# Attention scores from two scaled float16 pieces, with pairs of heads in the two row halves of the TensorE array

## The chip, the cores and the metric

The kernel runs on one core of one Trainium2 chip. Its time is the device time of one execution in microseconds. Three runs of the kernel before gave 969.35, 967.27 and 971.53 us, median 969.35.

## The reference

The input x is 1,024 tokens by 512 features, all in float32. Four blocks follow each other, each of the form x + layernorm(f(layernorm(x))):

1. causal attention with 32 heads of 16 features, 8 groups of 4 heads; the heads of a group share keys and values. Scores are q.k / 4, the upper triangle is masked, then softmax, weighted sum, output projection and a bias;
2. a gated feed-forward layer with ternary weights and 1,792 hidden features;
3. an attention by autocorrelation over Fourier transforms, with the six largest lags;
4. a gated feed-forward layer with 1,376 hidden features and low-rank additions to its weights.

```
q = (x @ Wq).reshape(t, 32, 16);  kv = (x @ Wkv).reshape(t, 8, 2, 16)
scores = einsum('bhqd,bhkd->bhqk', q, k)          # k of head h is that of group h // 4
weights = softmax(where(causal, -inf, scores) * (1 / 16 ** 0.5))
ctx = einsum('bhqk,bhkd->bhqd', weights, v);  out = ctx @ Wo + bo
```

The change touches block 1 alone, and there the scores.

## The kernel before

**Scores in pieces.** A float32 product of q and k is made in 16-bit operands: q and k are each split into three bfloat16 pieces, and of the nine products of pieces the six in `TERMS` (L11) are kept. A head has 16 features, so six terms stack into 96 contraction rows. `qt6` holds the stacked queries of three groups of heads in a ring, with the four heads beside each other in the free dimension, `kt6` the stacked keys of all groups. Every score is computed twice. `scores` (L1306) gives tiles of 128 queries by up to 512 keys, of which VectorE takes the row maxima (`row_max`, L1217). `scores_t` (L1324) gives the same transposed, 128 keys by queries, over 99 rows: three more rows hold the negative maxima of the queries in three pieces against rows of ones in `kt6`, so that the maximum is subtracted by the matmul. ScalarE makes the exponentials of those (L1300), GpSimd masks the diagonal block (L1208), and `weighted` (L1339) sums values by weight. In `weighted` the four heads lie in four column quarters of the array, and each float32 matmul is two instructions.

**Order in a group.** A group of four heads has eight stages, one for each tile of 128 keys (`kt`). `pe_group` (L1359) writes TensorE's order out by hand. In stages 0 to 3 each head has the slots S, ST, S, ST: two score matmuls of the row tile that is 14 steps ahead (`ahead`, L1259; so of the next group, or the one after it from stage 2 on) and two halves of the transposed scores of this stage; in stages 4 to 7 it has S, ST. Some slots, by `SUM_SLOTS` (L1379), carry a part of the weighted sum of the stage before: 1, 4, 4, 3, 3, 2, 2 and 1 in the eight stages. A score matmul waits until VectorE has taken the one two before (two PSUM banks); a transposed one waits until ScalarE has taken the one two before (two double banks). After stage 1, `max_pieces` (L1240) makes the pieces of the maxima on VectorE, and SyncE transposes them and brings them into `qt6` over DRAM. `for_groups` (L1113) writes out groups 0, 6 and 7 and runs a loop over groups 1 to 5 on every engine. Group 6 has scores ahead in stages 0 and 1 alone, group 7 in none.

**Before the groups.** LayerNorm on VectorE (L1468 to L1476), 32 transposes on TensorE, then projections (L1547): j = 0 the keys, then the values, j = 1 to 4 the queries. For each projection ScalarE makes piece 0 (L1518), VectorE a remainder and pieces 1 and 2 (L1486 to L1490); SyncE stores the three and loads the stacked rows (L1397 to L1408, `load_q` L1126). The ring is refilled at the start of each group for the second one after it. Beside this run 38 jobs that add the low-rank products to the weights of block 4 (`lora_job`, L949): matmul, copy on ScalarE, addition on GpSimd, a load and a store by DMA from ScalarE's queue. Their pieces (`lora_pieces`, L512) come from VectorE between xn and the first projection's pieces. The jobs are threaded between projections and 80 score matmuls of groups 0 and 1 that are made early. The groups begin when all jobs are copied and all early scores taken.

**What the other queues hold.** GpSimd fills rows 96 to 127 of `kt6` with ones (L1446) behind the wait for x and the start of a DMA. ScalarE's queue holds the low-rank loads and stores among its copies.

## Time and profile before

| | before |
|---|---|
| median of three runs | 969.35 us |
| span of the profiled execution | 966.3 us (no separate time of it is given) |
| instructions | 14,696 |
| busy share of TensorE, VectorE, ScalarE, GpSimd | 81%, 60%, 35%, 27% |
| L1321, scores | x384, 135.0 us busy |
| L1330, transposed scores | x384, 125.7 us busy |
| L1353, weighted sums | x1280, 100.4 us busy |
| L1300, exponentials | x256, 163.4 us busy |
| L1233 and L1237, row maxima | x256 and x128, 122.0 and 88.2 us busy |
| DMA | 94.16 MB, 144,473 packets |

Busy times add up what lies side by side: matmuls are pipelined and their ends are modelled, so that the starts of consecutive matmuls say more than their durations. A window is a stretch of the span; its row gives the busy time of each engine in it and the granted clock of TensorE as a share of full speed (1.00 is 2.4 GHz, 0.50 is 1.2 GHz).

### The profile page before, as it was taken

What the parts mean: (1) busy time and instruction counts of PE and PEld (TensorE: products, weight loads), DVE (VectorE), ACT (ScalarE), POOL (GpSimd) and SP (SyncE); (2) the same over time, 40 slices, a digit from 0 to 9 for tenths busy, and PEclk for the clock granted to TensorE, in tenths of its full rate; (3) what the DMA queues carried; (4) which work ended last, traced back from release to release, by engine and by line L of the source; (5) the groups of instructions that cost most, each with busy time, mean ns of one, the idle gap of its engine ahead of it and who ended that gap; (6) DMA issues with size and microseconds to landing.
All of it is one profiled execution on the core that took longest, in us unless ns stands there. A gap on an engine that the chain in (4) does not pass through costs nothing.

```text
span 966.3 us, 14696 instructions
## 1 busy us (share of the span) xinstructions
PE 782.0 (81%) x4174; PEld 317.3 (33%) x4174; DVE 579.3 (60%) x1433; ACT 338.6 (35%) x544; POOL 261.6 (27%) x248
## 2 busy tenths in 40 slices
PE   1957667988998989887499926998757799999993
PEld 1622222222322322223244412453323344444441
DVE  7524776767677677004999998136999815722004
ACT  1122225655556456760033301447203322212220
POOL 3024452121212202321034412434301114323221
PEclk9978558999889999997889967999978899999997
DMA  9498988612312124522206667103997400201001
GB/s 267 84 194 283 263 243 205 114 27 47 67 29 45 38 48 100 94 56 79 44 13 171 200 107 218 56 1 73 149 215 148 80 9 0 44 1 44 0 1 43
DMA packets 144473, 94.16 MB, mean 97 GB/s; under 512 B 110184, under 2 KB 123368, under 8 KB 144216
## 3 DMA queue, kind: packets, MB, share of 16 engines
q1 hardware_dynamic: 133376, 71.24, 33.4%
q10 hardware_dynamic: 10816, 16.91, 5.6%
q0 software_dynamic: 240, 5.51, 2.7%
q8 instruction: 21, 0.34, 0.1%
q14 instruction: 20, 0.16, 0.1%
HBM read 49.51 MB, written 29.04 MB: 81 GB/s over the span
## 4 chain that ended last, share of the span: by engine, by line
PE 54%; DVE 16%; DMA 10%; issue 8%; SPq 5%; ACT 3%; POOL 2%; DVEq 0%; ACTq 0%; POOLq 0%
PE ps L1077 19%; PE ps L1089 8%; PE ps L1353 8%; PE ps L1321 7%; PE ps L1330 5%; PE ps L1063 5%; DVE mx L1237 3%; DMA lorad_d<-arena 2%; DMA lora_d<-arena 2%; SPq L334 2%; DMA qp_d<-arena 1%; DMA arena<-arena 1%; DVE arena L1233 1%; DVE stats L460 1%; DVE arena L500 1%
## 5 line engine op out<-in xcount | busy, mean ns | idle before, releaser
L1077 PE MATMUL ps<-arena 128*128 128x512 f16 (+1 forms) x976 | 224.7, 388 | 40.4 <-issue 22.6
L1300 ACT ACTIVATE arena<-ps 128x1024 f32<-128x1024 f32 (+7 forms) x256 | 163.4, 651 | 116.4 <-PE ps L1330 111.6
L1321 PE MATMUL ps<-arena 96*128 (+4 forms) x384 | 135.0, 377 | 37.9 <-DVE mx L1237 16.5
L1233 DVE CUSTOM_DVE_ANT_0 arena<-ps,arena 128x256 bf16<-128x256 f32 (+3 forms) x256 | 122.0, 488 | 58.1 <-PE ps L1321 50.0
L924 POOL TENSOR_TENSOR arena<-arena (+2 forms) x50 | 67.4, 1349 | 307.3 <-ACT arena L856 299.5
L1077 PEld LDWEIGHTS ps<-arena 128*128 (+2 forms) x976 | 97.7, 101 | 161.2 <-issue 54.2
L1330 PE MATMUL ps<-arena 99*128 (+4 forms) x384 | 125.7, 344 | 4.6 <-ACT arena L1300 4.2
L1089 PE MATMUL ps<-arena 128*128 (+3 forms) x488 | 114.6, 384 | 11.3 <-POOL arena L929 10.9
L1237 DVE TENSOR_REDUCE mx<-ps 128x1 f32<-128x512 f32 x128 | 88.2, 689 | 27.2 <-PE ps L1321 26.3
L1353 PE MATMUL ps<-arena 128*32 128x256 f32 (+1 forms) x1280 | 100.4, 387 | 2.8 <-POOL arena L1208 2.2
L1208 POOL TENSOR_SCALAR_AFFINE_SELECT arena<-arena 128x512 f32<-128x512 f32 x64 | 40.7, 635 | 225.5 <-ACT arena L1300 225.2
L1063 PE MATMUL ps<-arena 128*128 128x512 f16 (+1 forms) x384 | 77.7, 364 | 23.8 <-DMA arena<-arena 16.0
L1321 PEld LDWEIGHTS ps<-arena 96*128 (+1 forms) x384 | 39.2, 102 | 148.3 <-issue 78.8
L1089 PEld LDWEIGHTS ps<-arena 128*128 (+2 forms) x488 | 47.6, 98 | 72.8 <-POOL arena L929 11.8
L682 DVE TENSOR_TENSOR arena<-ps,row_b 128x512 f32<-128x512 f32 x16 | 10.8, 678 | 95.8 <-PE ps L1089 95.8
L891 POOL TENSOR_TENSOR arena<-arena 128x512 f32<-128x512 f32 (+2 forms) x38 | 43.1, 1138 | 88.0 <-ACT arena L747 49.5
L929 POOL TENSOR_TENSOR arena<-arena (+2 forms) x50 | 61.6, 1236 | 0.0
L1063 PEld LDWEIGHTS ps<-arena 128*128 128x128 f16 x384 | 38.1, 100 | 63.1 <-DMA arena<-arena 17.0
L855 ACT ACTIVATE arena<-ps,gs (+2 forms) x22 | 15.1, 687 | 123.5 <-PE ps L1077 123.4
L855 ACT ACTIVATE arena<-ps,sc (+1 forms) x28 | 19.2, 687 | 104.8 <-PE ps L1077 104.8
L1330 PEld LDWEIGHTS ps<-arena 99*128 (+1 forms) x384 | 36.5, 99 | 40.0 <-issue 15.9
L1551 PE MATMUL ps<-arena 128*128 128x512 f32 x80 | 43.2, 671 | 6.1 <-DMA arena<-arena 5.3
(144 smaller groups left out, 735.7 us busy)
## 6 DMA issues: line engine op xcount, KB each, us to landing
arena<-qp_d SPq DMA_DIRECT2D x48, 128.0 KB, 4.4
lora_d<-arena ACTq DMA_DIRECT2D x20, 256.0 KB, 4.7
arena<-lora_d SPq DMA_DIRECT2D x10, 512.0 KB, 4.2
w1n_d<-arena SPq DMA_DIRECT2D x10, 512.0 KB, 3.1
arena<-rec_d SPq DMA_DIRECT2D x32, 128.0 KB, 2.6
qp_d<-arena SPq DMA_DIRECT2D x12, 256.0 KB, 4.1
w1dn_d<-arena SPq DMA_DIRECT2D x4, 704.0 KB, 3.2
arena<-in_L_ffn_down_w_dram ACTq DMA_DIRECT2D x16, 172.0 KB, 3.4
```

The costliest lines, as they stand in the source:

```text
L924: nc.gpsimd.tensor_tensor(hs[0:h, n % 2, :], sg[0:h, n % 2, :], u_sb[0:h, n % 2, :], ALU.mult).then_inc(hs_ready, 1)
L929: nc.gpsimd.tensor_tensor(hid[0:h, 1, n % 2, :], hs[0:h, n % 2, :], hid[0:h, 0, n % 2, :], ALU.subtract).then_inc(hid_ready, 1)
L1063: last = nc.tensor.matmul(to, lhs(w, kt), rhs(r, kt), start=(kt, w, r) == (0, 0, 0), stop=(kt, w, r) == (ND - 1, 1, 0))
L1077: last = nc.tensor.matmul(ps[0:h, 2 * (n % 2) + o, :], w(t[0])[:, kt, bass.ds(ht * P, h)], xt[:, c, t[1], kt, :], start=(kt, t) == (0, ter ...
L1089: last = nc.tensor.matmul(ps[:, 4 + i, :], hid[0:h, t[0], n % 2, i * P:(i + 1) * P], down(t[1])[0:h, ht, :], start=first and t == down_ter ...
L1233: nc.vector.tensor_tensor_reduce(out=junk[:, h, 0:w], in0=s_bank(g, u)[:, 0:w], in1=strip[:, D - w:D], scale=1.0, scalar=3.0 * NEG, op0=AL ...
L1237: nc.vector.reduce_max(mx[:, h, qt:qt + 1], s_bank(g, u)[:, 0:w], mybir.AxisListType.X).then_inc(s_taken, 1)
L1300: nc.scalar.activation(probs[:, kt % 2, h, kt * P:T], st_bank(h).rearrange("p b n -> p (b n)")[:, kt * P:T], ACT.Exp, scale=HD ** -0.5).th ...
L1321: nc.tensor.matmul(s_bank(g, u)[:, 0:k1 - k0], qt6[0:QROWS, g % RING, h, qt * P:(qt + 1) * P], kt6[0:QROWS, g, k0:k1], start=True, stop=Tr ...
L1330: last = nc.tensor.matmul(st_bank(h)[:, b, q0 - b * 512:512], kt6[0:QROWS + MROWS, g, kt * P:(kt + 1) * P], qt6[0:QROWS + MROWS, g % RING, ...
L1353: last = nc.tensor.matmul(o_bank[32 * h:32 * h + 32, b, q0 - b * 512:q1 - b * 512], vcur[:, kt, :], probs[:, kt % 2, h, q0:q1], start=kt = ...
L1551: last = nc.tensor.matmul(ps[:, 2 + 2 * (j % 2) + half, :], weights(c), xnt[:, c, half * 512:(half + 1) * 512], start=c == 0, stop=c == ND ...
```

## The change

- Queries and keys are split into two float16 pieces instead of three bfloat16 pieces, and three products of pieces are kept instead of six: 48 contraction rows, 51 with the maxima. The low-rank matrices keep their six terms (`LORA_TERMS`).
- The projections are scaled by powers of two, drawn from the largest weight of Wq and of Wk: two reductions on VectorE, a matmul that turns the result, one that spreads it over the partitions, and eight small operations. The scale of the exponential is now a tile of one number per partition (`escale`).
- The four heads of a group share the array's rows: heads 0 and 1 in rows 0 to 50, heads 2 and 3 in rows 64 to 114; the keys stand in both halves. The order of the heads is (2, 0, 3, 1) for the scores and (0, 2, 1, 3) for the transposed ones; a score matmul and the transposed one behind it lie in opposite halves.
- The maxima are divided by 2^14 and the rows of ones hold 2^14. They come by two DMAs instead of one.
- VectorE makes one pass for each projection instead of three; SyncE stores two pieces instead of three. The queries of a group come by six DMAs of 64 KB (before: six of 128 KB), the keys by six of 256 KB, as before.
- The fill of `kt6` covers all of it, and stands ahead of GpSimd's wait for x; SyncE waits for it before the key loads.
- On TensorE all eight groups are written out, with no loop; the other engines keep theirs.

```diff
-TERMS = ((0, 0), (0, 1), (1, 0), (1, 1), (0, 2), (2, 0))
+TERMS = ((0, 0), (0, 1), (1, 0))
 QROWS = HD * len(TERMS)
 MROWS = 3
+HALF = P // 2
+LORA_TERMS = ((0, 0), (0, 1), (1, 0), (1, 1), (0, 2), (2, 0))
+LROWS = HD * len(LORA_TERMS)
+S_ORDER, T_ORDER = (2, 0, 3, 1), (0, 2, 1, 3)
+MAX_SHIFT = 2.0 ** 14
...
-        pc = [room(16 + 4 * i, [2, T], BF16) for i in range(3)]
-        res = room(28, [2, T])
+        pc = [room(16 + 4 * i, [2, T], F16) for i in range(2)]
-        qt6 = room(112, [RING, REP, T], BF16)
-        kt6 = room(136, [G, T], BF16)
+        qt6 = room(112, [RING, REP // 2, T], F16)
+        kt6 = room(136, [G, T], F16)
...
+        def projection_scale(j):
+
+            return wscale[:, 0:1] if j else wscale[:, 1:2]
+
+        def projection_scales(dve, link):
+
+            dve.wait_ge(wq_loaded, 16)
+            nc.vector.tensor_reduce(wtop[:, 0:1], wq.rearrange("p c n -> p (c n)"), mybir.AxisListType.X, ALU.max,
+                                    apply_absolute_value=True).then_inc(wtop_ready, 1)
+            dve.wait_ge(wk_ready, 1)
+            nc.vector.tensor_reduce(wtop[:, 1:2], wk.rearrange("p c n -> p (c n)"), mybir.AxisListType.X, ALU.max,
+                                    apply_absolute_value=True).then_inc(wtop_ready, 1)
+            dve.wait_ge(wtop_turned, 1)
+            link(nc.vector.tensor_reduce(wexp[0:2, 0:1], ps[0:2, 0, 0:P], mybir.AxisListType.X, ALU.max))
+            dve.wait_ge(ident_ready, 1)
+            nc.vector.tensor_scalar(wdiag[0:2, :], ident[0:2, 0:2], wexp[0:2, 0:1], None, ALU.mult).then_inc(wdiag_ready, 1)
+            dve.wait_ge(wtop_spread, 1)
+            link(nc.vector.tensor_copy(wexp[:, :], ps[:, 1, 0:2]))
+            exponent(link, wexp[:, :], wexp[:, :], 2.0 ** -60)
+            inverse_of(link, wscale[:, :], wexp[:, :], 2)
+            nc.vector.tensor_scalar(escale[:, :], wexp[:, 0:1], wexp[:, 1:2], HD ** -0.5 / 16,
+                                    ALU.mult, ALU.mult).then_inc(scale_ready, 1)
+            dve.wait_ge(scale_ready, 1)
...
         def load_q(sp, g):
 
-            for s, (qp, _) in enumerate(TERMS):
-                src = qp_d[qp].rearrange("(g h d) t -> g d h t", g=G, h=REP)
-                sp.dma_start(qt6[HD * s:HD * (s + 1), g % RING, :, :], src[g]).then_inc(qt_loaded, 16)
+            for r in range(2):
+                for s, (qp, _) in enumerate(TERMS):
+                    src = qp_d[qp].rearrange("(g r s d) t -> g r d s t", g=G, r=2, s=2)
+                    at = HALF * r + HD * s
+                    sp.dma_start(qt6[at:at + HD, g % RING, :, :], src[g, r]).then_inc(qt_loaded, 16)
...
-                sp.dma_start(qt6[QROWS:QROWS + MROWS, g % RING, :, :],
-                             mt_d[g, 0:MROWS * REP * NT, :].rearrange("(i r) q -> i (r q)", i=MROWS)
-                             .rearrange("i (h t) -> i h t", h=REP)).then_inc(m_loaded, 16)
+                for r in range(2):
+                    at = HALF * r + QROWS
+                    src = mt_d[g, 0:MROWS * REP * NT, :].rearrange("(i r s t) q -> r i s (t q)", i=MROWS, r=2, s=2)
+                    sp.dma_start(qt6[at:at + MROWS, g % RING, :, :], src[r]).then_inc(m_loaded, 16)
...
-            n(nc.vector.tensor_scalar(p3[:, 0], mx[:, :, :], -1.0, None, ALU.mult))
-            n(nc.vector.scalar_tensor_tensor(out=mr[:, :, :], in0=mx[:, :, :], scalar=-1.0, in1=p3[:, 0],
+            n(nc.vector.tensor_scalar(p3[:, 0], mx[:, :, :], -1.0 / MAX_SHIFT, None, ALU.mult))
+            n(nc.vector.scalar_tensor_tensor(out=mr[:, :, :], in0=mx[:, :, :], scalar=-1.0 / MAX_SHIFT, in1=p3[:, 0],
...
-                for h in range(REP):
-                    n = 32 * g + 4 * kt + h
+                for k, h in enumerate(T_ORDER):
+                    n = 32 * g + 4 * kt + k
                     act.wait_ge(st_ready, n + 1)
-                    if h == 0 and (kt >= 2 or shape > 0):
+                    if k == 0 and (kt >= 2 or shape > 0):
                         act.wait_ge(pv_done, NT * g + kt - 1)
                     nc.scalar.activation(probs[:, kt % 2, h, kt * P:T],
-                                         st_bank(h).rearrange("p b n -> p (b n)")[:, kt * P:T],
-                                         ACT.Exp, scale=HD ** -0.5).then_inc(p_ready, 1)
-                    if (kt, h) == OUT_STEP and shape > 0:
+                                         st_bank(k).rearrange("p b n -> p (b n)")[:, kt * P:T],
+                                         ACT.Exp, scale=escale[:, 0:1]).then_inc(p_ready, 1)
+                    if (kt, k) == OUT_STEP and shape > 0:
                         take_o(act, g - 1)
 
...
-            nc.tensor.matmul(s_bank(g, u)[:, 0:k1 - k0], qt6[0:QROWS, g % RING, h, qt * P:(qt + 1) * P],
-                             kt6[0:QROWS, g, k0:k1], start=True, stop=True).then_inc(s_ready, 1)
-
-        def scores_t(pe, g, kt, h, b, shape):
-
-            n = 4 * kt + h
+            rows = slice(HALF * (h // 2), HALF * (h // 2) + QROWS)
+            nc.tensor.matmul(s_bank(g, u)[:, 0:k1 - k0], qt6[rows, g % RING, h % 2, qt * P:(qt + 1) * P],
+                             kt6[rows, g, k0:k1], start=True, stop=True).then_inc(s_ready, 1)
+
...
-            last = nc.tensor.matmul(st_bank(h)[:, b, q0 - b * 512:512], kt6[0:QROWS + MROWS, g, kt * P:(kt + 1) * P],
-                                    qt6[0:QROWS + MROWS, g % RING, h, q0:q1], start=True, stop=True)
+            last = nc.tensor.matmul(st_bank(k)[:, b, q0 - b * 512:512], kt6[rows, g, kt * P:(kt + 1) * P],
+                                    qt6[rows, g % RING, h % 2, q0:q1], start=True, stop=True)
...
-                    h, half = divmod(slot, halves)
+                    k, half = divmod(slot, halves)
                     if to:
-                        scores(pe, *to, h, half, False)
-                    scores_t(pe, g, kt, h, half if halves == 2 else 1, shape)
+                        scores(pe, *to, S_ORDER[k], half, False)
+                    scores_t(pe, g, kt, k, half if halves == 2 else 1, shape)
...
-                for i in range(3):
+                for i in range(2):
                     dst = kp_d[i] if j == 0 else qp_d[i, (j - 1) * P:j * P, :]
                     sp.dma_start(dst, pc[i][:, j % 2, :]).then_inc(pieces_stored[j % 2], 16)
                 if j == 0:
-                    sp.wait_ge(pieces_stored[0], 48)
-                    for s, (_, kp) in enumerate(TERMS):
-                        sp.dma_start(kt6[HD * s:HD * (s + 1), :, :],
-                                     kp_d[kp].rearrange("(g d) t -> d g t", g=G)).then_inc(kt_loaded, 16)
+                    sp.wait_ge(pieces_stored[0], 32)
+                    sp.wait_ge(ones_ready, 1)
+                    for r in range(2):
+                        for s, (_, kp) in enumerate(TERMS):
+                            at = HALF * r + HD * s
+                            sp.dma_start(kt6[at:at + HD, :, :],
+                                         kp_d[kp].rearrange("(g d) t -> d g t", g=G)).then_inc(kt_loaded, 16)
...
+            nc.gpsimd.memset(kt6[:, :, :], MAX_SHIFT).then_inc(ones_ready, 1)
...
-            nc.gpsimd.memset(kt6[QROWS:P, :, :], 1.0).then_inc(ones_ready, 1)
-            pool.wait_ge(ones_ready, 1)
...
+            projection_scales(dve, link)
...
-                nc.vector.tensor_tensor(res[:, b, :], ps[:, 2 + 2 * b:4 + 2 * b, :].rearrange("p b n -> p (b n)"), pc[0][:, b, :],
-                                        ALU.subtract).then_inc(res_ready, 1)
-                dve.wait_ge(res_ready, j + 1)
-                link(nc.vector.tensor_copy(pc[1][:, b, :], res[:, b, :]))
-                nc.vector.tensor_tensor(pc[2][:, b, :], res[:, b, :], pc[1][:, b, :], ALU.subtract).then_inc(pieces_ready, 1)
+                nc.vector.scalar_tensor_tensor(out=pc[1][:, b, :], in0=ps[:, 2 + 2 * b:4 + 2 * b, :].rearrange("p b n -> p (b n)"),
+                                               scalar=projection_scale(j), in1=pc[0][:, b, :],
+                                               op0=ALU.mult, op1=ALU.subtract).then_inc(pieces_ready, 1)
...
-                nc.scalar.copy(pc[0][:, b, :], ps[:, 2 + 2 * b:4 + 2 * b, :].rearrange("p b n -> p (b n)")).then_inc(piece0, 1)
+                if j == 0:
+                    act.wait_ge(scale_ready, 1)
+                nc.scalar.activation(pc[0][:, b, :], ps[:, 2 + 2 * b:4 + 2 * b, :].rearrange("p b n -> p (b n)"), ACT.Copy,
+                                     scale=projection_scale(j)).then_inc(piece0, 1)
...
+            def weight_bounds(i):
+
+                if i == 0:
+                    pe.wait_ge(wtop_ready, 2)
+                    nc.tensor.matmul(ps[0:2, 0, 0:P], wtop[:, :], ident[:, :], start=True, stop=True).then_inc(wtop_turned, 1)
+                if i == 5:
+                    pe.wait_ge(wdiag_ready, 1)
+                    nc.tensor.matmul(ps[:, 1, 0:2], wones[0:2, :], wdiag[0:2, :], start=True, stop=True).then_inc(wtop_spread, 1)
+
             pe.wait_ge(wk_ready, 1)
-            project(0, lambda c: wk[:, c, :], lambda i: None)
+            project(0, lambda c: wk[:, c, :], weight_bounds)
             for t in range(NT):
...
-            pe.wait_ge(ones_ready, 1)
-            for_groups(pe, pe_group)
+            for g in range(G):
+                pe_group(pe, g, g)
```

## Rows read from the trace of the kernel before

**Rows 1.** Windows, four of the eight groups: us, busy (instructions) by engine, PEclk, DMA share, GB/s.
```profile
222.00:260.00 38.00, 33.76 (x257) 10.79 (x256) 27.35 (x86) 21.40 (x33) 7.39 (x11) 0.96 0.22 45
260.00:300.00 40.00, 36.56 (x259) 11.25 (x258) 27.51 (x87) 21.41 (x33) 8.25 (x11) 0.87 0.23 43
...
376.00:405.00 29.00, 26.70 (x225) 7.61 (x223) 11.32 (x30) 21.28 (x34) 7.74 (x11) 1.00 0.40 91
405.00:434.20 29.20, 23.58 (x214) 6.91 (x214) 0.35 (x1) 20.18 (x33) 7.79 (x11) 0.94 0.49 92
```

**Rows 2.** Windows, group 0 from stage 1 on; the last is stage 0 of group 1.
```profile
155.10:161.10 6.00, 5.93 (x49) 1.71 (x48) 4.75 (x15) 3.67 (x4) 0.90 (x3) 1.00 0.98 210
161.10:167.90 6.80, 5.23 (x49) 1.62 (x48) 5.20 (x16) 3.24 (x4) 0.60 (x1) 1.00 0.88 187
167.90:172.50 4.60, 4.43 (x40) 1.50 (x39) 3.33 (x12) 2.81 (x4) 0.67 (x2) 1.00 0.09 17
172.50:176.10 3.60, 3.60 (x34) 0.93 (x32) 2.71 (x8) 2.28 (x4) 0.60 (x1) 1.00 0.68 152
176.10:179.00 2.90, 2.69 (x25) 0.78 (x25) 2.17 (x8) 1.94 (x4) 0.64 (x2) 1.00 1.33 150
179.00:181.70 2.70, 2.31 (x27) 0.81 (x26) 1.64 (x8) 1.43 (x5) 0.66 (x2) 1.00 1.27 290
181.70:183.80 2.10, 1.88 (x16) 0.70 (x16) 1.23 (x9) 1.11 (x4) 0.62 (x2) 1.00 0.22 49
183.80:190.20 6.40, 5.64 (x27) 1.72 (x26) 5.76 (x13) 4.90 (x5) 0.67 (x2) 1.00 0.85 126
```

**Rows 3.** Timeline of TensorE: start, us, line, operands, count; key projection, then one slot.
```profile
27.11 7.13 PE L1551 MATMUL ps<-arena 128*128 128x512 f32 x16 [0.78 <-ACT arena L1508]
...
206.82 0.39 PE L1321 MATMUL ps<-arena 96*128 x1
207.04 0.22 PE L1330 MATMUL ps<-arena 99*128 x1
...
207.19 0.38 PE L1330 MATMUL ps<-arena 99*128 x1
207.50 0.64 PE L1353 MATMUL ps<-arena 128*32 128x256 f32 x8
208.08 0.39 PE L1321 MATMUL ps<-arena 96*128 x1
```

**Rows 4.** Timeline of TensorE at the start of stage 2, in group 1.
```profile
198.22 0.39 PE L1321 MATMUL ps<-arena 96*128 x1 [1.86 <-DVE mx L1237]
```

**Rows 5.** Groups of instructions, ScalarE: line, operands, count | busy us, mean ns | idle before.
```profile
L764 ACT ACTIVATE arena<-ps 128x512 f32<-128x512 f32 x8 | 4.8, 597 | 40.7 <-PE ps L1063 40.7
...
L856 ACT ACTIVATE arena<-ps,sc 128x512 f32<-128x512 f32 x11 | 7.5, 680 | 0.0
```

**Rows 6.** Windows, a stretch in stage 0 of group 3.
```profile
260.70:267.70 7.00, 7.00 (x24) 1.76 (x23) 4.92 (x13) 4.37 (x5) 0.00 (x0) 0.51 0.75 115
```

**Rows 7.** Chain that ended last, before the groups: start, us, what.
```profile
27.91 2.37 DMA arena<-in_L_ffn_down_a_dram
...
59.09 13.90 DMA qp_d<-arena
...
147.60 0.61 PE ps L1321
```

**Rows 8.** DMA from 40 to 160 us: totals.
```profile
DMA packets 22994, 28.68 MB, mean 239 GB/s; under 512 B 9247, under 2 KB 13343, under 8 KB 22911
```

**Rows 9.** Timeline of GpSimd, the fill of the key tile.
```profile
10.50 6.92 POOL L1446 MEMSET arena<- 32x8192 bf16 x1
```

**Rows 10.** Groups of instructions, VectorE.
```profile
L559 DVE TENSOR_REDUCE e<-arena 128x1024 f32 x8 | 9.7, 1214 | 0.1
...
L1473 DVE TENSOR_SCALAR var<-mv 128x8 f32<-128x8 f32 x1 | 5.0, 5047 | 0.0
...
L469 DVE TENSOR_SCALAR var<-mv 128x4 f32<-128x4 f32 x14 | 4.0, 289 | 0.5
```

More of the change, by code:

```diff
@@ L42, in unit @@
     before = sum(REP * len(chunks(row_tile(i))) for i in range(pos))
-    return before + len(chunks(row_tile(pos))) * h + c
+    return before + len(chunks(row_tile(pos))) * S_ORDER.index(h) + c
 def chunks(qt):
@@ L165, in build @@
         mr = sb("mr", [P, REP, NT])
-        m3 = sb("m3", [P, P], BF16)
-        mt = sb("mt", [P, P], BF16)
+        m3 = sb("m3", [P, P], F16)
+        mt = sb("mt", [P, P], F16)
+        wtop = sb("wtop", [P, 2])
+        wdiag = sb("wdiag", [P, 2])
+        wones = room(132, [P])
+        wscale = sb("wscale", [P, 2])
+        wexp = sb("wexp", [P, 2])
+        escale = sb("escale", [P, 1])
         dens = sb("dens", [P, 32])
@@ L175, in build @@
         nw = sb("nw", [P, 3, NT])
-        qp_d = dram("qp_d", [3, H * HD, T], BF16)
-        kp_d = dram("kp_d", [3, G * HD, T], BF16)
-        mt_d = dram("mt_d", [G, P, P], BF16)
+        qp_d = dram("qp_d", [2, H * HD, T], F16)
+        kp_d = dram("kp_d", [2, G * HD, T], F16)
+        mt_d = dram("mt_d", [G, P, P], F16)
         den_d = dram("den_d", [G, REP, T])
@@ L342, in sp_lora_stack @@
             sp.dma_start_transpose(lora_bt[:, :, :], lora_bs.rearrange("p n c -> p (n c)")).then_inc(lora_stacked, 16)
-            for t, (_, piece) in enumerate(TERMS):
+            for t, (_, piece) in enumerate(LORA_TERMS):
                 sp.dma_start(lora_at[RANK * t:RANK * (t + 1), :], lora_ap[0:RANK, piece, :]).then_inc(lora_stacked, 16)
@@ L515, in lora_pieces @@
             b, r, p = lora_b[:, :, :], lora_bres[:, :, :], lora_bs.rearrange("p n (s r) -> p n s r", r=RANK)
-            slots = [[t for t in range(len(TERMS)) if TERMS[t][0] == piece] for piece in range(3)]
+            slots = [[t for t in range(len(LORA_TERMS)) if LORA_TERMS[t][0] == piece] for piece in range(3)]
             a, ar = lora_a[0:RANK, :], lora_ares[0:RANK, :]
@@ L957, in lora_job @@
             h, w = (height(m, n), D) if m < 2 else (P, FF1 // 4)
-            nc.tensor.matmul(ps[0:h, lora_bank(k), 0:w], lora_bt[0:QROWS, m * N1 + n, 0:h],
-                             lora_at[0:QROWS, A_AT[m] + j * w:A_AT[m] + (j + 1) * w], start=True, stop=True).then_inc(lora_ready, 1)
+            nc.tensor.matmul(ps[0:h, lora_bank(k), 0:w], lora_bt[0:LROWS, m * N1 + n, 0:h],
+                             lora_at[0:LROWS, A_AT[m] + j * w:A_AT[m] + (j + 1) * w], start=True, stop=True).then_inc(lora_ready, 1)
         def pe_rest(pe):
@@ L1219, in row_max @@
             qt = row_tile(pos)
-            for h in range(REP):
+            for h in S_ORDER:
                 for c, (k0, k1, diagonal) in enumerate(chunks(qt)):
@@ L1558, in _ @@
             early = [(g, pos, h, c) for g, last_pos in ((0, NT), (1, LEAD)) for pos in range(last_pos)
-                     for h in range(REP) for c in range(len(chunks(row_tile(pos))))]
+                     for h in S_ORDER for c in range(len(chunks(row_tile(pos))))]
             def early_scores():
```

37 lines of the change are left out of this document (21 added, 16 removed).

## The prediction

> **What bounds the kernel now.** I read the busy times by group of heads first, then the stages of one group, then single instructions, then the start of the kernel. The profile page gives a span of 966.3 us with TensorE busy 81%. The eight attention groups fill 147.6 to 434.2 us. Six of them have the scores of a later group threaded in and take 36.4, 38, 38, 40, 38 and 38 us; the seventh takes 29.0 and the last, with no scores threaded in, 29.2. In each TensorE is busy for most of the time, VectorE for 27 us of the first six and ScalarE for 21 of all [rows 1]. The stages of group 0, all at full clock, show where TensorE binds: in stages 1 and 3 to 5 it is busy nearly throughout, while in stage 2 a gap stands beside VectorE's 5.20 of 6.80 us, and in stage 0 of the next group VectorE (5.76 of 6.40) and ScalarE (4.90) are as full as TensorE [rows 2]. The order of starts inside one slot shows what TensorE pays: 512 columns of one score matmul hold the next back by 0.22 us, and the four heads' weighted sums take 0.09 us to be let in and 0.58 us to be passed [rows 3].
>
> **The change: pairing the heads.** A score matmul (L1321) and the transposed one behind it (L1330) will lie in opposite 64-row halves. If the halves run at once, a pair costs the longer of the two. In stages 0 to 3 a head has two such pairs of 512 columns against w = 512, 384, 256, 128, so 2w columns vanish; in stages 4 to 7 one pair of w against w, so w vanish. By 0.22 us for 512 columns [rows 3] that is, for four heads, 1.7, 1.3, 0.9, 0.4, 0.9, 0.65, 0.4 and 0.2 us, 6.5 us a group. What stays is capped stage by stage by the engines beside it [rows 2]:
> stage 1, 6.0 us: VectorE is busy 4.75, so at most 1.2; I take 1.0. Stage 2, 6.8 us: 0.9 less 0.1; I take 0.8. The chain on the maxima stays: TensorE stands idle 1.86 us before the first score of stage 2, while VectorE makes the pieces of the maxima [rows 4], in as many operations as before. Stage 3: 0.4. Stage 4, 3.6 us: ScalarE 2.28 now and 2.6 with the edit below; 0.6. Stage 5: 0.4. Stages 6 and 7 end on ScalarE soon; 0.3 together. Stage 0: VectorE-bound, nothing, and 0.1 lost to ScalarE. Sum: 3.4 us of saving a group. Overlap of unlike rows is not in this trace for row halves. It is for column quarters: eight passes of 256 columns, two for each of four heads, go by in 0.58 us. A pass of 512 such four-byte columns on the whole array takes 7.13 / 16 = 0.45 us, so one of 256 about 0.22 and eight in a row 1.8 us; the quarters run at three times that rate [rows 3]. Bounds: none of the 6.5 us, or all of it. I take the capped value.
>
> The exponentials (L1300) get their scale from a tile instead of a constant. Copies of 512 columns out of PSUM take 597 ns with a constant scale and 680 ns with one from a tile [rows 5], so 83 ns more for each of 256: 21 us of ScalarE, 0.33 us a stage. It is hidden where TensorE or VectorE is later (stages 1 to 4), and is already in the 0.1 and the small values above. Group 6 has scores in stages 0 and 1 only: 1.0 saved, and about 1.0 of its six score-free stages' 2.0 lost; nothing. Group 7 is score-free: of 8 x 0.33 = 2.7 us I put 1.5 on the path. Bounds for all of it: 0 and 21 us.
> The Trainium skill weighs in on both. Its page "TensorE: Matmul & The Clock Gate", section "Measured speedup vs the span model", has tiles in other rows start about 4 ns apart, which gives the 6.5 us in full and, under the same caps, the same 3.4; no row half runs in this trace. Its page "ScalarE: Activation LUTs", section "What ACT_TABLE_LOAD costs", charges about 93 ns for each pointer operand, so 24 us by its figure against 21 by the rows: a cost that speaks against the change.
>
> The clock. TensorE's granted clock falls to 0.51 for 260.7 to 267.7 us, although its rows are full, and group 3 takes 40.0 us for it [rows 6] [rows 1]. Group 0, which took 35.1 us from stage 1 to the next stage 0 with clock 1.00 throughout [rows 2], is about 3 us faster than the five behind it. A TensorE that finishes its pairs early idles more in stages 0 and 2, so it may drop more often; but a half clock in stage 0 costs less than now, since the pairs of a head then take 4 x 0.22 = 0.88 us beside VectorE's 1.2 or more. I charge 1 us more a group for groups 0 to 5. Bounds: minus 3 (no drops at all) and plus 11 (worked out under the rivals).
> The unrolled groups on TensorE (L1605) change neither order nor waits. The loop's back edge costs nothing that I can find; I take 0, with 0.5 us a group either way.
> Attention: 6 x (3.4 - 1) = 14.4 less 0 less 1.5, so 13 us earlier.
>
> **The change before the groups.** The lead-in ends with the first matmul of group 0 at 147.60, and the chain before it goes over DMAs, 13.90 us of it in one piece for the query pieces [rows 7]. Between 40 and 160 us the DMAs move 28.68 MB at a mean 239 GB/s [rows 8]. Two pieces instead of three drop 5 stores of 256 KB; six loads of a group's queries become six of 64 KB instead of 128 KB, 3 x 384 KB for groups 0 to 2; the key loads stay six of 256 KB. That is 2.4 MB, at 239 GB/s 10 us. Not all is on the chain; each group's SyncE issues stay six (and one more for the maxima, about 0.4 us, off the path). VectorE's three passes over each projection become one, hidden behind the DMAs, so 0.
> The fill of the key tile moves to the front of GpSimd's queue. Now its 6.92 us [rows 9] overlap a VectorE operation on 128x8 numbers that takes 5.05 us, where its like on 128x4 takes 0.289 [rows 10]. That stall of 4.8 us should go. Behind it come xn, the transposes, the key projection; but the low-rank pieces start only when their last input has landed at 30.3 us [rows 7], and SyncE's transposes wait for those. So the 4.8 us pay only for the added work: two reductions of 2,048 and 512 columns on VectorE (an estimate of 2.4 and 0.6 us from 1.21 us for 1,024 in L559 [rows 10]), two tiny matmuls between those of the key projection, and about eight small operations of 0.2 to 0.3 us. VectorE waits for the sixth matmul of the projection (some 5 us after its first, which stands at 27.11 now [rows 3] and would at about 22.3), so it is through by about 29, ahead of 30.3. ScalarE's new wait for the scales stands before its first piece, which needs the whole key projection (to about 29.4) anyway; queued behind it are the copy of V and the first loads of the low-rank jobs, now at 41.4, so 0. SyncE's new wait on the fill is over by about 10 us, 40 us before it is reached. If the stall stayed, the pieces would start 3.3 us later, and everything behind them. I take 8 us earlier for the whole lead-in; bounds 3 us later and 12 earlier.
>
> **Sum.** 966.3 - 12.9 - 8 = 945.4 us of span. The page gives no separate time of the profiled execution; its span lies 3.05 us under the median of the three runs (969.35, from 967.27 to 971.53). Carried over, 948 us. Behind 434.2 us nothing is touched; it should shift as a block.
>
> **Rivals.**
> Full use, and a steadier clock: the half-clock stretches go (5 x 3 us and the 6 us that I charged), and the lead-in gives 12: 948 - 21 - 4 = 923. For it: only group 0 of the first six is free of them, and a half clock costs nothing in stage 0 once it is VectorE's. Against: less work on TensorE, more idling.
> The halves take turns: no pairing. Then -8 for the lead-in and a third of ScalarE's 21 us on the path: 969.35 - 8 + 7 = 968. For it: nothing here runs two row halves; against: the column quarters overlap.
> The lead-in gives nothing, since low-rank stores hold it: 956.
> The other side, the clock: from stage 1 to 3 TensorE needs 4.4, 4.4 and 3.8 us a stage once paired (8 x 0.22 a stage, plus 0.67 for each of 4, 4 and 3 sums). At half clock these double, 12.6 us more a group of which about 1.5 fall into slack: 11 us. Held through half of those stages in six groups it costs 5 us a group more than forecast, 948 + 30 = 978. It decides when a group loses 3.6 us more than forecast (21 / 6), so about 7 us more of TensorE-bound time at half clock. For it: the drops of rows 6 come where TensorE had just idled, and idling grows. Against: group 0 went through the same idling without a drop.
>
> **Chances.** Forecast 0.50, steadier clock 0.20, taking turns 0.13, lead-in nothing 0.09, clock lost 0.08. The range 922 to 968 leaves the clock case out and cuts into the two cases at its ends. About 0.5%, 5 us, is what a measurement of this kernel can tell. Faster: the forecast, the steadier clock, the lead-in case and a quarter of the halves case, 0.82. Same: the rest of that case less a little, 0.09. Slower: the clock and a little of the halves case, 0.09.
>
> **What would show it.** Pairs right: L1321 and the L1330 behind it start within some tens of ns in opposite halves; wrong if 0.22 us lie between them still. Stages 1 and 4 shrink most, stage 0 not. L1300 on 1,024 columns about 1.11 us instead of 1.03. Clock by group about 0.9 to 0.96; under 0.8 the rival is there. The 5.05 us operation falls under 0.5. The first matmul of group 0 near 140 us, the last of the groups near 413. I am wrong if the block behind the groups changes its length by more than a few us, or if VectorE turns out to leave stages 1 and 3 no room.

## The result, and the profile after

The changed kernel takes **992.1 us** (989.2 to 994.2 in four runs) against 970.4 us (967.3 to 973.7) for the kernel before beside it: ratio 1.023, 95% interval 1.020 to 1.026. It is 22 us slower, where I had forecast 21 us faster. The profiled executions have spans of 992.5 and 966.3 us, 26.2 apart. A run that lies more than 1.5% above the fastest of its kernel is left out of the comparisons below.

The windows of the whole groups first, as in [rows 1]: us, busy (instructions) of PE, PEld, DVE, ACT, POOL, then PEclk, DMA share, GB/s. These are groups 2, 3, 6 and 7 of the changed kernel, and all that follows them.
```profile
217.60:258.80 41.20, 35.09 (x260) 8.00 (x256) 27.32 (x86) 24.19 (x33) 7.62 (x10) 0.63 0.14 33
258.80:300.00 41.20, 35.13 (x260) 7.97 (x256) 27.32 (x86) 24.18 (x33) 7.61 (x10) 0.63 0.13 33
...
381.20:421.00 39.80, 36.41 (x229) 7.95 (x225) 12.02 (x32) 23.86 (x33) 7.66 (x10) 0.52 0.37 79
421.00:461.80 40.80, 35.90 (x225) 7.80 (x217) 0.35 (x1) 24.10 (x34) 8.29 (x11) 0.50 0.26 59
...
461.80:992.50 530.70, 437.68 (x1920) 197.60 (x1912) 320.36 (x682) 137.32 (x227) 151.06 (x117) 0.92 0.34 77
```
The clock is the column to look at: 0.63 where it was 0.96 and 0.87, and 0.50 to 0.52 in the last two groups where it was 1.00 and 0.94. Those two, which have few scores (group 6) or none (group 7) and so few pairs or none, grew most, by 10.8 and 11.6 us, and in them TensorE is busy for 91% and 88% of the time at the lower of its two levels, 1.2 GHz. What follows the groups took 532.1 us before and takes 530.7.

The stages of group 0 from stage 1 on, and stage 0 of group 1, answering to [rows 2]:
```profile
144.45:152.30 7.85, 7.72 (x49) 1.49 (x48) 4.81 (x15) 4.03 (x4) 0.87 (x2) 0.50 0.96 207
152.30:161.10 8.80, 7.68 (x52) 1.49 (x48) 5.14 (x15) 3.60 (x4) 0.64 (x1) 0.50 0.50 106
161.10:167.10 6.00, 5.33 (x41) 1.19 (x40) 3.59 (x12) 3.18 (x4) 0.66 (x2) 0.50 0.79 172
167.10:170.80 3.70, 3.29 (x34) 0.78 (x32) 2.74 (x9) 2.83 (x5) 0.64 (x2) 0.92 1.02 232
170.80:173.30 2.50, 2.29 (x24) 0.70 (x24) 2.08 (x8) 1.98 (x4) 0.61 (x1) 1.00 0.00 0
173.30:175.75 2.45, 1.87 (x24) 0.70 (x24) 1.65 (x8) 1.90 (x5) 0.64 (x1) 1.00 0.00 0
175.75:177.94 2.19, 1.51 (x18) 0.53 (x18) 1.29 (x9) 1.35 (x4) 0.64 (x2) 1.00 0.00 0
177.94:184.13 6.19, 4.41 (x26) 1.11 (x26) 5.56 (x13) 5.26 (x5) 0.64 (x2) 0.77 0.22 66
```
Stages 1 to 3 stand at 0.50 and are longer (7.85, 8.80, 6.00 against 6.0, 6.8, 4.6); stages 5 and 6, at 1.00, are shorter (2.50 and 2.45 against 2.9 and 2.7); stages 4 and 7 are as long as before (3.70 and 2.19 against 3.6 and 2.1). The pairing pays in some of the stages where the clock holds.

The two matmuls of a pair do run at once. TensorE's timeline at full clock: start, us, line, operands. Scores (L1361) and transposed scores (L1371) start together, where the second came 0.22 us later in [rows 3]; the pair takes 0.32 us to the weighted sums.
```profile
208.87 0.39 PE L1361 MATMUL ps<-arena 48*128 48x512 f16 x1
208.87 0.39 PE L1371 MATMUL ps<-arena 51*128 51x512 f16 x1
209.19 0.64 PE L1394 MATMUL ps<-arena 128*32 128x256 f32 x8
```
The start of the groups on the same timeline, the operation that stalled behind the fill, and the longest exponentials (groups of instructions: count | busy us, mean ns | idle before):
```profile
135.80 0.61 PE L1361 MATMUL ps<-arena 48*128 48x512 f16 x1 [4.39 <-ACT arena L783]
```
```profile
L1517 DVE TENSOR_SCALAR var<-mv 128x8 f32<-128x8 f32 x1 | 0.2, 171 | 0.0
```
```profile
L1339 ACT ACTIVATE arena<-ps,escale 128x1024 f32<-128x1024 f32 x32 | 35.6, 1118 | 15.0 <-PE ps L1371 10.7 <-DMA lorad_d<-arena 4.0
```
Group 0 starts at 135.80 us, 11.8 before the 147.60 of [rows 7]; the 5.05 us operation of [rows 10] takes 0.17. So the spans differ by -11.8 in the lead-in, +39.4 in the groups (286.6 to 326.0) and -1.4 behind them: +26.2.

### The profile page after: what moved, and what is told of

The parts are those of the page before. It is cut to its first block, busy times and chain, and to the rows that moved or that the text cites. A ratio compares the mean times of both kernels' runs of the same rounds, so it can differ in the third digit from the quotient of the medians.

```text
span 992.5 us, 13933 instructions
## 1 busy us (share of the span) xinstructions
PE 811.7 (82%) x4178; PEld 300.6 (30%) x4178; DVE 569.3 (57%) x1433; ACT 362.0 (36%) x544; POOL 262.2 (26%) x248
## 4 chain that ended last, share of the span: by engine, by line
PE 56%; DVE 15%; DMA 9%; issue 9%; SPq 4%; ACT 3%; POOL 2%; DVEq 0%; ACTq 0%; POOLq 0%
PE ps L1113 19%; PE ps L1394 12%; PE ps L1125 8%; PE ps L1361 6%; PE ps L1099 5%; PE ps L1371 4%; DMA lora_d<-arena 4%; DVE mx L1276 2%; DMA lorad_d<-arena 2%; SPq L346 2%; DMA arena<-arena 2%; DVE arena L1272 1%; DVE stats L472 1%; ACT arena L1339 1%; DVE arena L512 1%
## 5 line engine op out<-in xcount | busy, mean ns | idle before, releaser
L1113 PE MATMUL ps<-arena 128*128 128x512 f16 (+1 forms) x976 | 222.9, 386 | 37.7 <-issue 22.4
L1339 ACT ACTIVATE arena<-ps,escale 128x1024 f32<-128x1024 f32 (+7 forms) x256 | 186.2, 741 | 133.0 <-PE ps L1371 126.3
L1361 PE MATMUL ps<-arena 48*128 48x512 f16 (+3 forms) x384 | 153.3, 457 | 46.0 <-DVE mx L1276 19.6
L1371 PE MATMUL ps<-arena 51*128 51x512 f16 (+3 forms) x384 | 153.1, 462 | 6.2 <-ACT arena L1339 6.1
L1394 PE MATMUL ps<-arena 128*32 128x256 f32 (+1 forms) x1280 | 140.2, 525 | 2.8 <-POOL arena L1247 1.6
L1125 PE MATMUL ps<-arena 128*128 (+3 forms) x488 | 116.3, 388 | 11.6 <-POOL arena L965 11.3
L1361 PEld LDWEIGHTS ps<-arena 48*128 48x128 f16 x384 | 32.6, 100 | 185.2 <-DVE mx L1272 91.7
L1394 PEld LDWEIGHTS ps<-arena 128*32 128x32 f32 x1280 | 30.2, 130 | 67.5 <-issue 55.4
```

Source lines behind the costliest of these rows:

```text
L1113: last = nc.tensor.matmul(ps[0:h, 2 * (n % 2) + o, :], w(t[0])[:, kt, bass.ds(ht * P, h)], xt[:, c, t[1], kt, :], start=(kt, t) == (0, ter ...
L1125: last = nc.tensor.matmul(ps[:, 4 + i, :], hid[0:h, t[0], n % 2, i * P:(i + 1) * P], down(t[1])[0:h, ht, :], start=first and t == down_ter ...
L1339: nc.scalar.activation(probs[:, kt % 2, h, kt * P:T], st_bank(k).rearrange("p b n -> p (b n)")[:, kt * P:T], ACT.Exp, scale=escale[:, 0:1] ...
L1361: nc.tensor.matmul(s_bank(g, u)[:, 0:k1 - k0], qt6[rows, g % RING, h % 2, qt * P:(qt + 1) * P], kt6[rows, g, k0:k1], start=True, stop=True ...
L1371: last = nc.tensor.matmul(st_bank(k)[:, b, q0 - b * 512:512], kt6[rows, g, kt * P:(kt + 1) * P], qt6[rows, g % RING, h % 2, q0:q1], start= ...
L1394: last = nc.tensor.matmul(o_bank[32 * h:32 * h + 32, b, q0 - b * 512:q1 - b * 512], vcur[:, kt, :], probs[:, kt % 2, h, q0:q1], start=kt = ...
```

## The experiments

The diffs show only the lines that make the difference; the loads, waits, tiles and fills that follow from them are left out. "The lower level" is a granted clock of 0.50, and the height of a matmul is the number of rows that it addresses.

**Theory 1**: TensorE's clock is lost because the score matmuls address only 48 or 51 rows of the array; what holds the clock is rows at work over time. **Rival 2**: pairs end early, TensorE idles, and idling loses it. **Rival 3**: the loop written out. **Rival 4**: float16 or the values. **Rival 5**: the slower exponential stretches the stages.

**1. The products on the full height, no pairs.**
```diff
-TERMS = ((0, 0), (0, 1), (1, 0))
+TERMS = ((0, 0), (0, 1), (1, 0)) * 2
-            rows = slice(HALF * (h // 2), HALF * (h // 2) + QROWS)
+            rows = slice(0, QROWS)
```


> The changed kernel with its score and transposed-score matmuls back on the whole height of the array: the three products stand twice, in rows 0 to 47 and 48 to 95, the scale in the exponential is halved for it, the maxima lie in rows 96 to 98, and no two matmuls share the array. Float16, two pieces, the scales from the weights, the exponential's scale from a tile and the unrolled groups all stay. Theory 1 (the clock is lost because the score matmuls fill only 48 or 51 rows of one half, so that the array does less in each us): the granted clock of groups 0 to 7 returns to 0.93-1.00, groups 6 and 7 to 29-30 us each, and the time is that of before less the lead-in's 10 us and up to 3 us more for the slower exponential: 958-966 us. Rival 2 (pairs end early and TensorE idles in between): the same here, 958-966. Rival 3 (the unrolled loop) and rival 4 (float16, or the values in it): clock stays at 0.5-0.67, time 990-1030 us.

954.3 us, ratio to before 0.981 (0.976 to 0.987), 4 us under the range that theory 1 and rival 2 gave. Groups 1 to 6 have clock 0.95 to 1.00, and group 6 takes 29.2 us again; groups 0 and 7 stand at 0.83 and 0.80, lower than expected. Float16, the written-out loop and the slower exponential are all in this kernel, so none of them loses the clock by itself: rivals 3 and 4 fall. Rival 2 stands yet.

**2. Pairs in the same half.**
```diff
-S_ORDER, T_ORDER = (2, 0, 3, 1), (0, 2, 1, 3)
+S_ORDER, T_ORDER = (0, 2, 1, 3), (0, 2, 1, 3)
```


> The changed kernel with the heads of the scores taken in the order 0, 2, 1, 3 instead of 2, 0, 3, 1, the same order as the transposed ones, so that the two matmuls of a slot stand in the same half of the array and run one after the other; rows, data and counts stay. Theory 1 (few rows at a time): the rows in use are still 48 or 51 at once, so the clock of groups 0 to 5 stays at 0.50-0.67 or falls further, groups 6 and 7 stay near 40 us each, and without the overlap the time grows to 1010-1060 us. Rival 2 (overlap makes TensorE idle, and idling loses the clock): without overlap TensorE is as busy as before, the clock returns to 0.93-1.00 and the time is 958-972 us.

1051.1 us (1049.8 to 1052.3 in three runs), ratio 1.080 (1.074 to 1.087). A fourth run took 3,840 us with clock 1.00; why is not known, and it is left out. A window over two groups and the start of a third:
```profile
192.63:300.00 107.37, 101.83 (x547) 21.78 (x545) 58.10 (x181) 51.02 (x69) 16.17 (x22) 0.50 0.11 26
```
TensorE is busy for 95% of it at the lower level. Rival 2 falls: more busy time, less clock. The Trainium skill's page "TensorE: Matmul & The Clock Gate", section "What's actually happening", has the gate set by how busy the array has been; by busy time alone this kernel would stand at full clock, and the measurement decides against that reading.

**3. The kernel before with the loop written out.**
```diff
-            for_groups(pe, pe_group)
+            for g in range(G):
+                pe_group(pe, g, g)
```


> The kernel before with one edit, TensorE's loop over the eight groups written out as in the changed kernel. Rival 3 (the code written out loses the clock or stalls TensorE's instruction stream): the granted clock of the groups falls below 0.8 and the time is over 980 us. Theory 1 and rival 2: the clock stays at 0.93-1.00 in the groups and the time is within 3 us of before, 967-973 us.

965.3 us (955.0 to 967.2 in three runs), ratio 0.987 (0.979 to 0.995): a little faster, which none of the theories said; the clock of groups 1 to 5 is 0.83 to 1.00. So rival 3 falls here too. The loop's price is taken up in run 12.

**4. A constant scale in the exponential.**
```diff
-                                         ACT.Exp, scale=escale[:, 0:1]).then_inc(p_ready, 1)
+                                         ACT.Exp, scale=HD ** -0.5 / 2.0 ** 16).then_inc(p_ready, 1)
```


> The changed kernel with a constant in place of the tile as the exponential's scale, so that the scale drawn from the weights is left out of it and the probabilities are other numbers; the rest stays. Rival 5 (the slower exponential, 741 against 651 ns, stretches the stages, TensorE waits more, and loses the clock): clock of groups 0 to 5 back above 0.9, groups 6 and 7 to 30 us, time 955-965 us. Theory 1 (few rows at a time): the clock of groups 0 to 5 stays at 0.60-0.70, groups 6 and 7 at 39-41 us, and the time moves by at most 6 us, to 986-992 us.

The constant is not the number that the tile holds, so the probabilities differ a little from the changed kernel's. 975.2 us, ratio 1.002 (0.998 to 1.005), 17 us under the changed kernel and outside both expectations. Groups 1 to 5 keep clock 0.62 to 0.67 and 40.5 to 41.1 us each, as theory 1 says, so rival 5 is not the cause. But the last two groups come back part of the way:
```profile
379.70:411.80 32.10, 28.95 (x221) 7.26 (x221) 12.03 (x32) 20.69 (x33) 7.61 (x10) 0.72 0.39 85
411.80:437.90 26.10, 23.68 (x183) 5.87 (x179) 0.35 (x1) 18.67 (x26) 5.79 (x8) 0.75 0.42 96
```
With 2.8 us less of ScalarE a group they run at 0.72 and 0.75 against 0.52 and 0.50. Neither theory had this; the slower exponential seems to have a part in keeping the clock low there, and how is open.

**5. Full height, the added rows zero.** Rows 48 to 95 are zero on the queries' side, the maxima in 96 to 98.
```diff
+            rows = slice(0, PAD)            # PAD = 96, scores
+            rows = slice(0, PAD + MROWS)    # transposed
```


> As the full-height kernel before it, but rows 48 to 95 hold no second copy of the products: the queries' side is zero there and the keys' side a constant, and only the maxima stand in rows 96 to 98; the queries' loads are half as many bytes. Theory 1 in the form that rows addressed count, whatever they hold: clock 0.93-1.00 in groups 1 to 7 and 948-958 us, like the full-height kernel's 954. Theory 1 in the form that what the rows hold counts (products of zero do nothing): the score matmuls are as thin as 48 rows and run one after the other, clock 0.5-0.67 in all groups, 1030-1055 us like the 1052 of the kernel with both matmuls in one half.

951.0 us, ratio 0.979 (0.973 to 0.986), clock 0.90 to 0.95 in groups 0 to 5. Group 3:
```profile
242.00:279.10 37.10, 32.81 (x257) 9.62 (x256) 27.14 (x87) 23.98 (x34) 7.62 (x10) 0.95 0.16 36
```
Against run 2 the matmuls have the same columns and also run one after the other; 96 rows are addressed for 48, and the products of those added are all zero. So added rows bring the clock back although their products are zero.

**6. Short scores, full transposed scores.**
```diff
-            rows = slice(0, QROWS)
+            rows = slice(0, HD * len(TERMS) // 2)
```


> The full-height kernel with one edit: the score matmuls use rows 0 to 47 alone (the maxima are doubled to fit), the transposed ones keep 99 rows, and none share the array. If what counts is how many rows are at work over time, the clock of groups 0 to 5 lies between the full-height kernel's 0.95 and the 0.5-0.6 of the same-half kernel, 0.65-0.90, and groups 6 and 7, where nearly no scores are left, keep 1.00 and 29-30 us: 965-1005 us. If only a pair in two halves at once or the transposed matmuls' thinness loses the clock, groups 0 to 5 stay at 0.95 and the time at 952-958 us.

1107.7 us, ratio 1.141 (1.133 to 1.149): far outside what I expected, though on the side of theory 1. The clock is 0.50 from 213.1 to 300.0 us. It comes back in group 6 from stage 2 on, where only the transposed scores on 99 rows are left (0.95). A second cost shows as well. TensorE's timeline:
```profile
230.31 0.61 PE L1368 MATMUL ps<-arena 99*128 99x512 f16 x1
230.86 0.61 PE L1358 MATMUL ps<-arena 48*128 48x512 f16 x1
231.40 0.40 PE L1368 MATMUL ps<-arena 99*128 99x256 f16 x1
```
512 columns hold the next matmul back by 0.54 to 0.55 us when it has another height, against 0.40 to 0.43 at the same clock where both heights are of a kind (run 11). Each change costs some 0.11 to 0.15 us here, and a slot has up to two. The Trainium skill's page "TensorEngine Tiling (Array Packing)", section "Key Properties", says that a change of tiling mode, though not of tile, drains TensorE; these rows agree, and put a number to it.

**7. An extra matmul over all rows before each score matmul.**
```diff
+            if extra:
+                nc.tensor.matmul(s_bank(g, u)[:, 0:k1 - k0], qt6[:, g % RING, h % 2, qt * P:(qt + 1) * P],
+                                 kt6[:, g, k0:k1], start=True, stop=True)
```


> The changed kernel, its paired halves kept, with an extra matmul before each score matmul of the groups' slots: all 128 rows, the same columns into the same bank, overwritten by the score matmul behind it. It only adds work to TensorE, some 170 matmul-lengths of 110 to 213 ns at full clock for every two groups, and nobody needs its result. Theory 1 (few rows at work over time loses the clock): the clock of groups 0 to 5 returns to 0.90-1.00 and the time falls below the changed kernel's 992, to 955-975 us, although TensorE does more. Against it (the clock falls with overlap, or with idle time that work at half clock doesn't have, or from anything else in the kernel): the clock stays, the extra matmuls cost 8-14 us a group at 1.2 GHz, and the time is over 1030 us.

1015.3 and 1025.5 us in the two runs that are left, so no interval. The time misses both expectations; the clock answers. Of groups 0 to 5, those of 42 to 44 us have 0.96 to 1.00 and those of 51 to 53 us 0.68 to 0.77, where the changed kernel has 0.61 to 0.67 in all. Useless full-height work brings much of the clock back, but costs more than that: 0.32 us for each 512 columns, for their 0.22 and a change of height.
```profile
233.77 0.39 PE L1363 MATMUL ps<-arena 128*128 128x512 f16 x1
234.09 0.39 PE L1365 MATMUL ps<-arena 48*128 48x512 f16 x1
```

**8. Run 1 with the constant scale.** The edit of run 4, with 17 for 16 in the exponent.

> The full-height kernel with a constant in place of the tile as the exponential's scale (the scale drawn from the weights is left out of it, and the probabilities are other numbers). At full clock the prediction's price for the slower exponential was 1.5 us, so 950-955 us; if the 90 ns of each exponential lie on the path in the stages as they did by 17 us at half clock, 935-942 us.

952.2 us, ratio 0.982 (0.973 to 0.992), against 954.3 in run 1: 2 us, within the scatter, where run 4 gained 17. What run 4 gained belongs to the low clock.

**9. Pairs kept, each matmul on all 64 rows of its half.**
```diff
+            rows = slice(HALF * (h // 2), HALF * (h // 2) + HALF)    # both matmuls
+                    sp.dma_start(qt6[at:at + MROWS, g % RING, :, :],
+                                 qt6[at + 8:at + 8 + MROWS, g % RING, :, :]).then_inc(m_cleared, 16)
```


> The changed kernel with its pairs, but each matmul of a pair addresses all 64 rows of its half; the rows behind the products (and behind the maxima) hold zero on the queries' side, and each reuse of a ring slot first clears its rows of maxima. A pair so addresses 128 rows instead of 99, for the same result. Theory 1 (rows addressed over time hold the clock): the clock of groups 0 to 5 rises above the changed kernel's 0.63-0.67, to 0.70-0.95, groups 6 and 7 above 0.5, and the time falls to 945-985 us. If more rows of the same half change nothing (what counts is that a matmul stands in one half), clock 0.63-0.67 and 988-996 us.

945.6 and 950.8 us in the two runs that are left, so no interval; their mean, 948.2, is 44 us less than the changed kernel, for 13 to 16 more rows a matmul that hold zeros on one side. The clock of groups 0 to 5 is 0.77 to 0.95, that of groups 6 and 7 0.94 and 0.69. Two of groups 0 to 5:
```profile
170.00:204.50 34.50, 27.54 (x264) 8.04 (x260) 26.76 (x86) 24.05 (x33) 7.59 (x10) 0.95 0.16 39
...
242.30:279.40 37.10, 30.89 (x256) 7.95 (x254) 26.73 (x84) 23.79 (x32) 7.26 (x10) 0.77 0.16 36
```

**10. Run 5 with the transposed scores on 128 rows.**
```diff
-            rows = slice(0, PAD + MROWS)
+            rows = slice(0, P)
```


> The zero-padded full-height kernel, with the transposed score matmuls on all 128 rows instead of 99 (the added rows are zero on the queries' side). Theory 1: the granted clock of groups 1 to 6, 0.91-0.95 there, rises to 0.97-1.00, and the time falls by 1-2 us a group, from 951 to 940-949 us. Without an effect of rows above 99: 949-953 us.

**942.3 us** (937.3 to 946.9, six runs), ratio 0.971 (0.966 to 0.976): the lowest median of the study, 29 us under the one before. Four of groups 1 to 5 stand at 1.00, where run 5 had 0.91 to 0.95 in all:
```profile
237.00:272.60 35.60, 31.31 (x258) 9.44 (x256) 27.09 (x87) 23.99 (x34) 7.59 (x10) 1.00 0.17 38
```
Most of the 29 us is not the clock's. Between the profiled spans, 966.3 and 935.6 us, lie 30.7 us: the groups begin at 127.92 instead of 147.60, which is 19.7; they and what ends them take 277.0 us instead of 286.6, which is 9.6; the rest, 1.4, lies behind. The groups of run 9 begin at 134.77, 1.0 before the changed kernel's, so its 44 us do lie in the groups.

**11. Run 5 with 66 and 69 rows.**
```diff
-PAD = 96
+PAD = 66
```


> The zero-padded full-height kernel with 66 and 69 rows instead of 96 and 99 (the maxima stand in rows 66 to 68), so that the matmuls still don't fit into one half. If the number of rows counts, the clock of groups 0 to 5 lies between 0.93 and the 0.5 of 48 rows in one half: 0.6-0.85, and 970-1030 us. If it is the use of a half that counts, not the rows, clock 0.9-0.95 and 949-955 us.

1064.3 us, ratio 1.094 (1.087 to 1.100), above the range that I gave for rows counting. A group of it, and TensorE's timeline:
```profile
244.35:297.53 53.18, 52.36 (x257) 13.39 (x256) 27.65 (x86) 24.28 (x33) 7.63 (x11) 0.50 0.12 25
```
```profile
253.37 0.61 PE L1360 MATMUL ps<-arena 66*128 66x512 f16 x1
253.77 0.42 PE L1370 MATMUL ps<-arena 69*128 69x256 f16 x1
```
These matmuls fit in no half, so it is not the use of a half that costs the clock. From 66 rows to 96, the added ones all zeros, the clock goes from 0.50 to between 0.90 and 0.95 and the time falls by 113 us; the groups begin at 128.99 and 129.72 us, so the lead-in has no part in it. `PAD` is the only edit between the two kernels.

**12. Run 5 with TensorE's loop rolled.** The edit of run 3 the other way round.

> The zero-padded full-height kernel with TensorE's loop over the groups rolled again for groups 1 to 5, as in the kernel before. The kernel before gained 6 us from the loop written out; if that gain is of the loop, this one is 3-8 us slower than 951: 954-959 us. If it was chance, 949-953 us.

955.4 us, ratio 0.983 (0.977 to 0.988), against 951.0: with run 3 (7 us by the medians) the second sign that the loop costs 4 to 7 us. Run 3's interval leaves 1 out, but some of its runs lie among those of the kernel before; the intervals of runs 5 and 12 overlap. It is likely, not shown.

## Why the prediction was wrong, point by point

**The lead-in**: predicted -8, with 12 as its end; measured -11.8. The stall went as I said. The weights' scales are ready at 29.9 us, before the key projection ends at 30.7; ScalarE's first piece starts at 30.75, and VectorE goes on at 30.52, when the last low-rank input has landed at 30.4. Where the 3.8 us beyond my 8 come from is not taken apart; run 1, which loads twice as many rows of queries and of keys as run 5, begins its groups at 139.03 us against 129.72, so the bytes loaded weigh.

**The pairing**: right in kind, and near in size as a sum, partly by luck. Group 1 of run 9, with pairs, and of run 10, without, give it at full clock on both sides. Run 9, stages 2 to 7 and the next stage 0:
```profile
183.82:190.59 6.77, 4.67 (x48) 1.40 (x48) 5.54 (x18) 3.60 (x4) 0.64 (x1) 1.00 0.03 6
190.59:194.89 4.30, 3.91 (x40) 1.33 (x40) 3.20 (x12) 3.17 (x4) 0.64 (x1) 1.00 0.48 127
194.89:198.03 3.14, 2.75 (x32) 0.76 (x30) 2.71 (x9) 2.78 (x5) 0.64 (x1) 1.00 0.08 22
198.03:200.95 2.92, 2.58 (x26) 0.80 (x26) 2.31 (x9) 2.35 (x5) 2.92 (x2) 1.00 0.00 0
200.95:203.01 2.06, 1.59 (x22) 0.61 (x23) 1.44 (x8) 1.55 (x5) 0.63 (x2) 1.00 0.21 32
203.01:205.19 2.18, 1.50 (x18) 0.52 (x18) 1.20 (x8) 1.40 (x4) 0.63 (x1) 1.00 0.55 90
205.19:211.51 6.32, 3.82 (x26) 1.08 (x26) 5.66 (x13) 5.15 (x5) 0.64 (x2) 1.00 0.25 66
```
Run 10, the same stages:
```profile
177.08:184.35 7.27, 5.32 (x49) 1.66 (x48) 5.75 (x17) 3.60 (x4) 0.64 (x2) 1.00 0.03 6
184.35:188.88 4.53, 4.17 (x39) 1.54 (x40) 3.20 (x12) 3.17 (x4) 0.63 (x1) 1.00 0.45 130
188.88:192.54 3.66, 3.66 (x34) 0.98 (x33) 2.75 (x9) 2.64 (x4) 0.64 (x1) 1.00 0.02 7
192.54:195.47 2.93, 2.72 (x26) 0.87 (x24) 2.13 (x8) 2.21 (x4) 2.93 (x3) 1.00 0.00 0
195.47:198.08 2.61, 2.21 (x27) 0.77 (x24) 1.64 (x8) 1.78 (x4) 0.62 (x2) 1.00 0.31 47
198.08:200.29 2.21, 1.85 (x17) 0.62 (x18) 1.20 (x8) 1.36 (x4) 0.64 (x2) 1.00 0.38 63
200.29:206.98 6.69, 5.48 (x26) 1.28 (x26) 5.83 (x14) 5.15 (x5) 0.63 (x1) 1.00 0.28 61
```
0.50, 0.23, 0.52, 0.01, 0.55, 0.03 and 0.37, together 2.2 us; I had 0.8, 0.4, 0.6, 0.4, then 0.3 for stages 6 and 7 together and -0.1 for stage 0, together 2.4. Of the terms only stage 4 fits: stage 5 gave nothing for my 0.4, stage 6 more than I had, and stage 0, which I called VectorE's, gave 0.37. The sum is no firmer than a few tenths: stages 2 to 7 give 1.8 us here and 1.6 in group 4 of the same two kernels (0.28, 0.24, 0.51, 0.01, 0.54, 0.03). Against the kernel before at full clock, the seven stages of [rows 2], it is 29.1 less 27.7, 1.4 us. Stage 1, where I put the last 1.0, stands at 0.55 to 0.75 in groups 0 to 5 of run 9, so it is not measured.

**The exponentials**: 90 ns each for the 83 of [rows 5] (1118 against 1028 on 1,024 columns), and 2 us at full clock (runs 1 and 8, within the scatter) for my 1.5. No error shows where the clock holds; in the changed kernel 17 us hang on it (run 4).

**The loop at nothing**: low, by some 4 to 7 us in the kernel's favour, as far as runs 3 and 12 tell.

**The clock: the step that failed.** "I charge 1 us more a group for groups 0 to 5", with bounds of -3 and +11, and for groups 6 and 7 nothing and 1.5. Measured are the 39.4 us that the groups lost in place of the 12.9 that they were to gain. Two things were wrong in it. I read the drops of [rows 6] as what idling does, and so gave them to stages in which TensorE would idle more. In the windows of runs 2, 6 and 11 TensorE is busy for 95 to 100% of the time and stands at 0.50 (run 11: 52.36 of 53.18 us); addressed rows of zeros bring the clock back (runs 5, 9 and 10). Halving the rows and halving the time of a pair are the same edit, and I priced only the second. And since I tied the loss to pairs, I left groups 6 and 7 out, which lost 22.4 of the 39.4 us: their transposed scores are as thin as the rest, and group 6 enters its stage 1 at the lower level. The rival "the other side, the clock", at 978 us and 0.08, had the right place for groups 0 to 5, the right sign and the right size: 5 us a group more than forecast, where 17.0 lost in place of 14.4 gained make 5.2. Its mechanism was idling too, and it left out groups 6 and 7. My own sign for it, a clock under 0.8 by group, came true.

Thin matmuls are not the whole of it. Stages 2 to 7 of group 6 hold the transposed scores and the weighted sums alone, and the same stages run at different levels:

| kernel | window | us | TensorE busy | rows of the transposed scores | clock of stage 1 | clock of stages 2 to 7 |
|---|---|---|---|---|---|---|
| before | 387.78:404.57 | 16.79 | 15.43 | 99 | 1.00 | 1.00 |
| changed | 396.87:422.26 | 25.39 | 24.01 | 51 | 0.50 | 0.50 |
| run 11 | 466.33:492.99 | 26.66 | 25.60 | 69 | 0.50 | 0.50 |
| run 6 | 524.38:542.59 | 18.21 | 16.71 | 99 | 0.50 | 0.95 |
| run 4 | 394.57:412.81 | 18.24 | 16.99 | 51 | 0.50 | 0.87 |
| run 7 | 440.02:457.02 | 17.00 | 15.43 | 51 | 1.00 | 1.00 |

Run 7 enters these stages at full clock, with its extra matmuls just behind it, and holds it on 51 rows. From the lower level, the changed kernel (51 rows) and run 11 (69) stay there and run 6 (99) comes back. But run 4, with its faster exponential, comes back on 51 rows, and so does run 7 within its group 7, from 0.50 (462.60 to 469.40 us) to 1.00 (475.30 to 478.60). So what went before seems to count as well; no run takes that apart.

That more rows addressed bring the clock back is shown by runs 5, 9, 10 and 11; that nothing else counts is not. Open are what lets run 4 recover in group 6 where the changed kernel doesn't (the exponential's scale is the only edit between them), and what pairing would give in stage 1.
